# A recurrence whose input sums are made eight steps at a time and placed with slices of the identity

## The reference

```python
xw = jnp.einsum('ntd,dh->nth', x, Wx) + b
def step(prev_h, xw_t):
    next_h = jnp.tanh(xw_t + prev_h @ Wh)
    return (next_h, next_h)
_, hs = jax.lax.scan(step, h0, jnp.swapaxes(xw, 0, 1))
```

## Time and profile before

| | us |
|---|---|
| median of 3 runs | 1146.18 |
| lowest and highest of them | 1141.81, 1150.68 |
| span of the profiled execution | 1136.0 |
| median less that span | 10.2 |
| busy: TensorE, its weight loads, VectorE, ScalarE, GpSimd | 1042.3, 782.3, 580.7, 547.1, 311.8 |

### The profile page before, as it was taken

How to read it: one execution, slowest core, us unless ns; L and a number is a source line. 1 busy time by engine, 2 the same in 40 slices (tenths; PEclk the granted TensorE clock), 3 DMA queues, 4 the chain that set the end, 5 groups by cost and what they waited for, 6 DMA issues and landing times.

```text
span 1136.0 us, 62532 instructions
## 1 busy us (share of the span) xinstructions
PE 1042.3 (92%) x26280; PEld 782.3 (69%) x26280; DVE 580.7 (51%) x1954; ACT 547.1 (48%) x1956; POOL 311.8 (27%) x308
## 2 busy tenths in 40 slices
PE   8899999999999999997798999999998999999994
PEld 5566666666666666666685444457888999999994
DVE  2333333333333333336585898998754655645641
ACT  2333333333333333337685777673344665665652
POOL 2111111111011111012240005437602455455455
PEclk7999999999999999999899999999999999999998
DMA  2121221122433333203861001104325566566644
GB/s 86 50 75 63 74 75 63 60 74 66 47 42 41 42 41 44 28 10 58 184 133 41 1 0 62 46 32 145 141 66 177 127 148 156 124 148 149 131 61 47
DMA packets 85349, 89.63 MB, mean 79 GB/s; under 512 B 8657, under 2 KB 71654, under 8 KB 85298
## 3 DMA queue, kind: packets, MB, share of 16 engines
q1 hardware_dynamic: 70706, 71.87, 25.2%
q0 software_dynamic: 14592, 17.10, 9.0%
HBM read 56.82 MB, written 33.96 MB: 80 GB/s over the span
## 4 chain that ended last, share of the span: by engine, by line
PE 64%; DVE 11%; ACT 9%; issue 7%; POOL 5%; DMA 2%; SPq 1%; POOLq 1%; DVEq 0%; ACTq 0%
PE ps L521 18%; PE ps L793 14%; PE ps L807 7%; DVE tok L1139 7%; PE ps L659 7%; ACT zt L859 6%; PE ps L500 4%; PE ps L503 3%; PE ps L709 2%; PE ps L490 2%; POOL slots_in L446 2%; PE ps L581 2%; PE ps L566 2%; PE ps L718 2%; POOL big L420 1%
## 5 line engine op out<-in xcount | busy, mean ns | idle before, releaser
L1139 DVE STREAM_TRANSPOSE tok<-zt 128x32 f32<-128x32 f32 x1024 | 159.6, 194 | 331.3 <-ACT zt L859 310.7
L859 ACT ACTIVATE zt<-ps 128x32 f32<-128x32 f32 x1024 | 146.2, 195 | 332.3 <-PE ps L521 332.3
L521 PE MATMUL ps<-wh,tok 128*8 128x64 f32 x8192 | 212.1, 222 | 43.4 <-DVE tok L1139 1.9
L500 PE MATMUL ps<-wx,xst 128*8 128x64 f32 x8320 | 217.7, 221 | 1.1 <-issue 1.1
L521 PEld LDWEIGHTS ps<-wh,tok 128*8 128x8 f32 x8192 | 118.1, 88 | 123.9 <-DVE tok L1139 110.3
L465 POOL DMA_INDIRECT out<-arena,dest x80 | 127.6, 1595 | 98.8 <-ACT arena L1017 79.6
L503 PE MATMUL ps<-brow,tri 1*8 1x64 f32 x4160 | 153.9, 217 | 0.7 <-issue 0.7
L500 PEld LDWEIGHTS ps<-wx,xst 128*8 128x8 f32 x8320 | 145.0, 91 | 4.7 <-issue 2.4
L793 PE MATMUL ps<-xgT_hi,ew_hi 128*128 128x320 f32 (+1 forms) x384 | 118.7, 309 | 4.1 <-DVE spare L1281 1.6
L793 PE MATMUL ps<-xgT_hi,ew_lo 128*128 128x320 f32 (+1 forms) x384 | 119.0, 310 | 0.0
L793 PE MATMUL ps<-xgT_lo,ew_hi 128*128 128x320 f32 (+1 forms) x384 | 118.2, 308 | 0.0
(11 more groups left out here) (206 smaller groups left out, 1754.6 us busy)
## 6 DMA issues: line engine op xcount, KB each, us to landing
ring<-k_pad SPq DMA_DIRECT2D x64, 256.0 KB, 6.2
slots_in<-mid SPq DMA_DIRECT2D x16, 645.0 KB, 3.3
mid<-slots_in SPq DMA_DIRECT2D x16, 645.0 KB, 4.2
arena<-in_ex_down SPq DMA_DIRECT2D x16, 384.0 KB, 3.2
arena<-in_ex_gate SPq DMA_DIRECT2D x16, 352.0 KB, 4.7
arena<-in_ex_up SPq DMA_DIRECT2D x16, 352.0 KB, 5.9
xst<-in_x_steps SPq DMA_DIRECT2D x66, 64.0 KB, 1.8
xtok<-in_x_tok SPq DMA_DIRECT2D x16, 256.0 KB, 2.7
```

The source lines that it names most:

```text
L500: nc.tensor.matmul(sums_at(bank, t)[Q * j:Q * j + B], xst[:, bank, k, t], wx[:, k, j * W:(j + 1) * W], start=t < 2 and k == 0, stop=False, ...
L521: last = nc.tensor.matmul(sums_at(bank, t)[Q * j:Q * j + B], hring[:, (n - 1) % (2 * G), k, 0:B], wh[:, k, j * W:(j + 1) * W], start=False ...
L859: nc.scalar.activation(zt[:, n % 2, half], sums_at(n // G, n % G)[:, half], ACT.Tanh).then_inc(s_zt, 1)
L1139: nc.vector.transpose(hring[:, n, k], zt[:, n % 2, k * Q:(k + 1) * Q]).then_inc(s_h, 1)
```

## The change

The input sums of a group of eight steps are made by two products (`inputs_summed`, one for each half of the 256 input features): 64 rows (8 steps x 8 sequences) by 256 columns, in PSUM bank 5, not tiled in column blocks. They are issued behind the steps t = 1 and t = 2 of the group before. At t = 5 VectorE adds the bias to them and writes them into `xw`, in the first 64 partitions of `spare` (`inputs_out`); the bias is loaded for that as 64 equal rows, and the other 64 partitions of `xw` are set to zero once. For each step `seed` then issues four products with the eight columns 8t to 8t + 7 of the identity, which put the step's eight rows into the four column tiles; they start the sum (start=True), and L521 adds to it. The seeds of step t + 1 are issued behind L521 of step t. The sums of a step lie in one of two banks by turns. The identity is loaded among the first, the triangle among the late ones.

The nine constants of `loads` are issued from ScalarE's queue, ahead of its table load, not from SyncE's.

```diff
-        first = ((wx, wx_d), (tri, tri_d), (brow, b_rec_d))
+        first = ((wx, wx_d), (ident, ident_d), (brow, b_rec_d))
...
-        def sums_at(group, t):
-
-            return ps[:, 2 * group + t % 2, t // 2 * W:(t // 2 + 1) * W]
+        def sums_at(t):
+
+            return ps[:, t % 2, 0:W]
...
             sp.dma_start(xst[:, 1], x_steps[1]).then_inc(s_xs[1], 16)
-            for dst, src in loads:
-                sp.dma_start(dst[:], src).then_inc(s_const, 16)
...
-            def xpart(bank, t):
-
-                for k in range(C):
-                    for j in range(J):
-                        nc.tensor.matmul(sums_at(bank, t)[Q * j:Q * j + B], xst[:, bank, k, t], wx[:, k, j * W:(j + 1) * W],
-                                         start=t < 2 and k == 0, stop=False, skip_group_check=True, tile_position=(0, Q * j))
+            def inputs_summed(bank, c):
+
+                return nc.tensor.matmul(ps[0:G * B, 5, 0:D], xst[:, bank, c].rearrange("p t b -> p (t b)"), wx[:, c], start=c == 0, stop=c == C - 1)
+
+            def seed(bank, t):
+
                 for j in range(J):
-                    last = nc.tensor.matmul(sums_at(bank, t)[Q * j:Q * j + B], tri[0:1, 1, 0:B], brow[:, j * W:(j + 1) * W],
-                                            start=False, stop=False, skip_group_check=True, tile_position=(0, Q * j))
-                return last
+                    nc.tensor.matmul(sums_at(t)[Q * j:Q * j + B], ident[:, B * t:B * t + B], xw[:, bank, j * W:j * W + W],
+                                     start=True, stop=False, skip_group_check=True, tile_position=(0, Q * j))
             for _ in range(WARM):
                 keep_up(512)
-            pe.wait_ge(s_ps0, 1)
             pe.wait_ge(s_first, FIRST_LOADED)
             pe.wait_ge(s_xs[0], 16)
-            for t in range(G):
-                last = xpart(0, t)
-            last.then_inc(s_xdone, 1)
+            inputs_summed(0, 0)
+            inputs_summed(0, 1).then_inc(s_xdone, 1)
+            pe.wait_ge(s_ps0, 1)
+            pe.wait_ge(s_xin, 1)
+            seed(0, 0)
...
                     last.then_inc(s_sum, 1)
-                    if t == 0:
+                    if t < G - 1:
+                        seed(bank, t + 1)
+                    else:
+                        pe.wait_ge(s_xin, 2 * i + bank + 2)
+                        seed(1 - bank, 0)
+                    if t == 1:
                         pe.wait_ge(s_xs[1 - bank], 16 * i + 16 + 16 * bank)
-                    last = xpart(1 - bank, t)
-                    if t == G - 1:
-                        last.then_inc(s_xdone, 1)
+                        inputs_summed(1 - bank, 0)
+                    if t == 2:
+                        inputs_summed(1 - bank, 1).then_inc(s_xdone, 1)
...
         def _(act):
+            for dst, src in loads:
+                act.dma_start(dst[:], src).then_inc(s_const, 16)
             act.preload_act_table(ACT.Tanh)
...
+            nc.vector.memset(xw[G * B:P], 0.0)
+
+            def inputs_out(done, bank):
+
+                dve.wait_ge(s_xdone, done)
+                nc.vector.tensor_tensor(xw[0:G * B, bank], ps[0:G * B, 5, 0:D], brow[:], ALU.add).then_inc(s_xin, 1)
+            dve.wait_ge(s_first, FIRST_LOADED)
+            inputs_out(1, 0)
...
                     turn(i, n)
+                    if n % G == 5:
+                        inputs_out(2 * i + n // G + 2, 1 - n // G)
```

## The result

The changed kernel takes 1184.76 us (median of 4 runs, 1178.24 to 1188.69) against 1145.66 for the kernel before (also four runs by now): the ratio is 1.0357, with a 95% interval of 1.0317 to 1.0396. It is slower, by about 39 us on the medians. The profiled execution has a span of 1178.8 us against 1136.0, 42.8 us more, and it took 1180.83 us: 2.0 us lie around its span, not the 10.2 that the prediction took from a median of other executions.

What follows compares the result with a forecast made beforehand. The prediction took the recurrence as a latency loop of 512 x 0.97 us. Span 1136.0 - 3.1 (start) + 2.6 (wide products) + 10.2 (around the span), about 1146, plus 33 for clock dips gave 1179; range 1138 to 1225.

Steps and rivals of the forecast that it cites:

- The loop is bound by latency, so the removed products give nothing at full clock: Recurrence: a 0.97 us latency loop hides the twelve removed products a step; gain 0, at most 79 us.
- The clock dips between pairs, about once in an iteration: Recurrence: thinned steps drop TensorE's clock until the next wide pair; 32 dips of 4 us cost 33 us, bounds 0 to 113.
- The low steps: Recurrence at half clock: a step takes 1.17 us, or 1.77 with a wide product.
- The wide products at full clock: Two in eight steps: the next L521 starts at 0.985 us against 0.97; 2.6 us in all, bounds 0 and 13.
- The sum on VectorE: Step 5 of each group: about 0.486 us by the nearest row, fits 0.66 us of idle time; cost 0.
- The start: Constants' loads on ScalarE's queue: first tanh 3.1 us earlier, at 8.9; bounds 0 and -3.1.
- The cover: Start of the kernel: TensorE's first work ends by 7.7 us, before the first tanh at 8.9.
- the clock holds because TensorE is never idle for long: Rival, recurrence: idle stretches of at most about 0.5 us keep the clock up; 1146 us, between 1140 and 1156, chance 0.36.
- The sentence of the Trainium skill: Rule that clock drops come from long idle gaps between bursts of matmuls; by it alone the sum stays at 1146.
- the clock stays down: Rival, recurrence: with 24 records a step the clock seldom or never returns; 1235 to 1325 us, chance 0.08.
- The shorter step: Rival, recurrence: L521 starts sooner behind a shorter queue, 0.02 us a step, 10 us; 1136 us, chance 0.06.

Runs made afterwards that it cites:

- e5_halves: The changed kernel with its two wide products cut into four half products behind steps 0, 2, 4 and 6; 1139.68 us, ratio 0.999 to the kernel before.
- e8_sp_loads: The changed kernel with the nine constants' loads back on SyncE's queue; 1181.59 us, ratio 1.0324 to the kernel before.
- e2_no_wide: The changed kernel without the loop's wide products, so it computes something else; 1217.99 us, ratio 1.0671 to the kernel before.
- e1_filler: The changed kernel with eight unused filler products a step in the six steps without a wide product; 1143.66 us, ratio 1.001 to the kernel before.
- e3_spread: The changed kernel with its two wide products behind steps 0 and 4 instead of 1 and 2; 1151.83 us, ratio 1.008 to the kernel before.
- e4_loads_only: The kernel before with only the nine constants' loads moved to ScalarE's queue; 1141.42 us, ratio 0.9994 to the kernel before.

## Why the prediction was right

The forecast was 1179, the measurement 1185, and the mechanism was the one forecast. How near the number came is in part luck, as its terms show. Point by point:

*The loop is bound by latency, so the removed products give nothing at full clock.* Shown: steps of 0.97 us with them, without them, and in e5_halves, which has 12,555 records in the window from 30 to 500 us where the kernel before has 19,767. The waits of the changed kernel from 30 to 515 us, beside the earlier trace rows:

```profile
ACT zt L866 <- PE ps L521: 331.7, 456, 1.5
...
PEld ps L521 <- DVE tok L1154: 259.9, 456, 0.8
```

The weight loads of L521 now wait 259.9 us for the transpose, not 106.4: the freed time became idle time.

*The clock dips between pairs, about once in an iteration.* Right in kind and place, and that the group with the kernel sums is spared is also seen: all 18 dips of the loop start at or near steps 7 and 8 and take in steps 9 and 10; the pair in steps 1 and 2 ran at full clock in every iteration but the first. The term was 32 dips of 4 us, 33 us in all. It was 18 dips of 6.8 us, and by the step times they cost 38 us: 36 steps of 1.80 instead of 1.03 are 28 us, the other 10 are steps of 1.18. So dips were fewer, longer, and dearer in each microsecond (31% of 122 us, not 26%), since they always held the pair. These errors nearly cancelled: 38 for 33.

*The low steps.* 1.18 and 1.80 us; the prediction had 1.17 and 1.77.

*The wide products at full clock.* The step takes 1.03, not 0.985: 0.055 late, not 0.015. One such step, just behind the low stretch shown above:

```profile
248.64 0.41 PE L521 MATMUL ps<-wh,tok 128*8 128x64 f32 x16 [0.45 <-DVE tok L1154]
...
249.10 0.65 PE L498 MATMUL ps<-wx,xst 128*64 128x256 f32 x2
...
249.67 0.41 PE L521 MATMUL ps<-wh,tok 128*8 128x64 f32 x16
```

Over 128 steps that is 7 us, where 2.6 were set; the cost of the dips above is counted on top of it, from 1.03. This term was mis-sized, inside its bound of 0.1. The wide product starts 0.46 behind L521, where the sum had 0.445, and L521 starts 0.57 behind the wide product, where it had 0.44 + 0.10.

*The sum on VectorE.* 64x256 from PSUM takes 0.396 us, in an idle stretch of 0.66, as said; nobody waits for it.

*The start.* 1.75 us earlier, not 3.1. The bounds held, the value was too good. The timeline of the changed kernel, beside the earlier trace rows:

```profile
4.57 0.45 ACTq L851 DMA_DIRECT2D rows_to<-in_rows_to  x1
...
6.75 1.08 PE L498 MATMUL ps<-wx,xst 128*64 128x256 f32 x4 [1.84 <-DMA brow<-in_b_rec]
...
8.77 0.26 ACT L854 ACTIVATE a_bc<-a_bc 128x64 f32<-128x64 f32 x1 [2.44 <-DMA rows_to<-in_rows_to]
...
10.22 0.27 ACT L866 ACTIVATE zt<-ps 128x32 f32<-128x32 f32 x2
```

ScalarE's nine issues end at 5.0, a microsecond earlier than estimated, but the last load lands 3.7 us later at 8.77, against 1.4 behind the last issue before. And TensorE's first wide product, which waits for the bias rows, starts at 6.75, not 4.84, which I had taken as given. With the loads back on SyncE's queue (e8_sp_loads) it starts at 5.21:

```profile
5.21 1.97 PE L500 MATMUL ps<-wx,xst 128*64 128x256 f32 x4 [0.30 <-DMA brow<-in_b_rec]
```

So 1.5 of the 1.9 us come with the second queue. The cover held all the same, by less than a microsecond: L521 ends at 9.3, the tanh was ready for it at 10.2.

*What offset this.* In the kernel before, the first 16 steps take 5.8 us more than 0.97 each: the first low stretch cost some 3 us (steps of 1.30) and three steps waited 0.7 to 1.0 us longer still, for a cause that was not looked into. In the changed kernel the first 16 steps take 1.8 us more than their 0.97 and 1.03, in a shorter low stretch, and none waits so. I had not counted these 4 us. With them the recurrence adds up: 38 for the dips, 7 for the wide products, less 4, is 41, and 41.1 were measured.

*The rivals.* That the clock holds because TensorE is never idle for long is out: at step 8 of the changed kernel TensorE's idle stretches are those ahead of L521, 0.35 to 0.45 us, the longest from 30 us to the last tanh is 0.47, and the clock fell 18 times. The sentence of the Trainium skill that was set against my reading (TensorE: Matmul & The Clock Gate, "Why this matters for your kernels") does not cover this case; the measurement decides. That the clock stays down is half seen in e2_no_wide, where the dense pairs are missing. The shorter step was not seen anywhere.

What is not settled: why the profiled stages behind the recurrence take 619.3 (e1_filler) to 629.0 us (e2_no_wide) in kernels that are the same there. The difference arises in the convolution, which ends 91 to 101 us behind the last tanh, where the clock also dips (6.8 us from 544.5 in the kernel before). It is as large as the spread of the times, and no experiment was made on it.

## What to carry to other kernels

TensorE works here in the shadow of a latency loop. Taking work from it saved nothing and cost the clock. In such a kernel, look at the granted clock of the thinnest stretch that the new schedule makes, not at the mean. If work is batched, spread it so that no long run of thin steps is left, in pieces small enough to fit beside the step's own products, as e5_halves does. If that can't be done, products that nobody reads can fill the thin steps: e1_filler won back about 40 us with them.

## What the runs showed of the hardware

The clock fell though TensorE's products never paused for more than 0.47 us in the loop (from 30 us on), behind steps busy 1.10 us of 2, and it rose again behind two wide products, and in e2_no_wide behind at most four steps with a few more small records. With the same products in other places (e3_spread) it did not fall between 24 us and the last tanh. Nine loads issued on a second queue beside the first went with later landings on the first: the hidden state's h0r was there at 7.76 us in e4_loads_only, by VectorE's copy of it, against 5.94 in the kernel before, and the bias rows at 6.75 in the changed kernel against 5.21 in e8_sp_loads, by the first wide product. Each of these is one profiled execution.
